# Expert tiles: gated rows turned one step later, second products two steps later, first products by half steps in three PSUM banks

## The reference

```python
x = x + 0.5 * ffn(layernorm(x))        # mixture of 8 experts, 2 chosen for each token
x = x + attention(layernorm(x))        # chunked delta-rule attention
x = x + 0.5 * ffn(layernorm(x))        # the same experts again

def ffn(xf):                           # for each expert e, w1 and w3: 256 x 128, w2: 128 x 256
    scores = softmax(xf @ gate_w); top_scores, top_idx = top_k(scores, 2)
    xs = scale[e] * xf                 # scale is the token's score for e, 0 if e was not chosen
    y += (silu(xs @ w1[e]) * (xs @ w3[e])) @ w2[e]
```

## Time and profile before

| | |
|---|---|
| median of three runs | 1602.56 us |
| profiled execution: span from first to last instruction | 1602.7 us |
| time around the span | none is given; the span is taken as the execution's time |
| TensorE busy (matrix multiplications) | 1349.0 us, 84% |
| VectorE / ScalarE / GpSimd busy | 1099.0 / 882.4 / 889.9 us |
| granted TensorE clock, mean | 0.929 of 2.4 GHz |
| gate function, 128x512, 72 times | 42.8 us busy, 154.3 us idle before it |

### The profile page before, as it was taken

How to read it: one execution, slowest core, us unless ns; L and a number is a source line. 1 busy time by engine, 2 the same in 40 slices (tenths; PEclk the granted TensorE clock), 3 DMA queues, 4 the chain that set the end, 5 groups by cost and what they waited for, 6 DMA issues and landing times. The chain is left out here.

```text
span 1602.7 us, 47314 instructions
## 1 busy us (share of the span) xinstructions
PE 1349.0 (84%) x17084; PEld 1208.4 (75%) x17084; DVE 1099.0 (69%) x2928; ACT 882.4 (55%) x1836; POOL 889.9 (56%) x1579
## 2 busy tenths in 40 slices
PE   7758888888557999999999999999997558878886
PEld 7757877877546888888888888878886457778775
DVE  7774454454376788989898998988984565543553
ACT  4424553455245777776676676676773335534552
POOL 3562455254536556657766676766757324562545
PEclk8978998998878999999999999999997779999998
DMA  8437663764101222222222222222223576537651
GB/s 249 161 115 228 215 202 122 266 212 159 57 22 25 42 51 47 52 60 71 74 63 68 67 70 64 75 70 65 71 56 81 169 222 221 192 152 246 207 179 60
DMA packets 218577, 193.42 MB, mean 121 GB/s; under 512 B 105188, under 2 KB 182250, under 8 KB 218352
## 3 DMA queue, kind: packets, MB, share of 16 engines
q1 hardware_dynamic: 184800, 114.06, 26.1%
q0 software_dynamic: 24576, 67.94, 11.5%
q10 hardware_dynamic: 8976, 8.40, 1.7%
HBM read 102.63 MB, written 94.01 MB: 123 GB/s over the span
## 5 line engine op out<-in xcount | busy, mean ns | idle before, releaser
L1734 DVE SCALAR_TENSOR_TENSOR raw_w<-attn_raw,taps,raw_w 128x256 f32<-128x256 f32 x576 | 240.9, 486 | 4.5 <-ACT raw_w L2143 4.5
L525 PE MATMUL ffn_both<-ws,ffn_xhi 128*128 x1152 | 211.7, 297 | 8.7 <-DVE ffn_xlo L743 3.8
L525 PEld LDWEIGHTS ffn_both<-ws,ffn_xhi 128*128 128x128 f32 x1152 | 170.9, 198 | 17.6 <-issue 17.2
L2421 POOL TENSOR_TENSOR attn_inv<-attn_inv,attn_term 64x14 f32<-64x14 f32 (+6 forms) x448 | 134.0, 299 | 35.1
L548 PE MATMUL ffn_yb<-ws,ffn_hhi 128*128 x576 | 132.0, 308 | 23.2 <-issue 14.7
L748 DVE TENSOR_TENSOR ffn_hid<-ffn_both,ffn_sil 128x512 f32<-128x512 f32 x72 | 49.6, 689 | 142.0 <-ACT ffn_sil L870 94.5
L2418 POOL TENSOR_TENSOR attn_term<-attn_small,attn_inv 64x14 f32<-64x14 f32 (+6 forms) x448 | 126.3, 282 | 32.6
L1334 PE MATMUL attn_fr<-attn_xhi,wqkv 128*128 128x256 f32 x768 | 139.3, 290 | 5.1 <-ACT attn_bth L2150 2.4
L870 ACT ACTIVATE ffn_sil<-ffn_both 128x512 f32<-128x512 f32 x72 | 42.8, 595 | 154.3 <-remote 108.0
L2460 POOL TENSOR_TENSOR attn_factors<-attn_squared,attn_powers 128x10 f32<-128x10 f32 x28 | 55.1, 1969 | 129.1 <-DVE attn_squared L1832 129.1
L548 PEld LDWEIGHTS ffn_yb<-ws,ffn_hhi 128*128 128x128 f32 x576 | 101.7, 204 | 32.8 <-issue 32.4
(11 more groups left out here) (342 smaller groups left out, 3904.0 us busy)
## 6 DMA issues: line engine op xcount, KB each, us to landing
ffn_xb<-second_rows SPq DMA_DIRECT2D x48, 259.0 KB
ffn_more_rows<-second_rows SPq DMA_DIRECT2D x48, 259.0 KB
raw_w<-second_rows SPq DMA_DIRECT2D x40, 259.0 KB
ffn_more_rows<-first_rows SPq DMA_DIRECT2D x64, 131.0 KB, 2.1
attn_xin<-x_after_first ACTq DMA_DIRECT2D x32, 256.0 KB, 2.7
attn_xres<-x_after_first SPq DMA_DIRECT2D x32, 256.0 KB
x_after_attention<-attn_xres SPq DMA_DIRECT2D x32, 256.0 KB
attn_xg<-x_after_attention SPq DMA_DIRECT2D x32, 256.0 KB, 3.1
```

The source lines that it names most:

```text
L525: last = pe.matmul(hp[:, j, :], (xhi, xlo)[b][:, k % 2, q, j * P:(j + 1) * P], ws[:, bass.ds(experts[j], 1), a, q].rearrange("p o d -> p ( ...
L1734: dve.scalar_tensor_tensor(acc[:, j, r], raw[:, j, r, :, tap:tap + P], taps[:, j, r, tap:tap + 1], acc[:, j, r], ALU.mult, ALU.add)\
L2421: pool.tensor_tensor(v[:, j + 1:, 0:j], v[:, j + 1:, 0:j], term[:, 0:k, 0:j], ALU.subtract)\
```

## The change

TensorE turns the gated rows of a step one step later and makes its second products two steps later. The first products are made in two half steps of two tiles each, each into one of three PSUM banks in turn (the third bank is `pos`, used only while tokens are being sent to experts). The gate function and the product with it are made by halves too, VectorE's and ScalarE's orders follow, and there are nine row buffers; the ninth takes the place of `xT`, which is used only while tokens are being sent to experts.

```diff
-        NW = 8
+        NW = 9
...
-        sil = sb("sil", [P, TPB, HF])
+        sil = sb("sil", [P, 2, TPB // 2, HF])
...
-        hp = both[:, 1].rearrange("p c t -> p (c t)").rearrange("p (j d) -> p j d", j=TPB)
+        hp = [t.rearrange("p (j d) -> p j d", j=TPB // 2) for t in (both[:, 1, 0], both[:, 1, 1], pos[:])]
...
             def up(k, experts, head):
-                wait(pe, sil_ready, k)
-                wait(pe, hid_ready, k)
+                wait(pe, hid_ready, 2 * k - 2)
...
                 for j in range(TPB):
-                    if head and j == TPB // 2:
-                        turn_rows(k + 1)
+                    n = 2 * k + j // 2
+                    if j == TPB // 2:
+                        if head:
+                            turn_rows(k + 1)
+                        wait(pe, hid_ready, n - 2)
...
-                last.then_inc(up_done, 1)
+                    if j % 2 == 1:
+                        last.then_inc(up_done, 1)
 
             def turn_hidden(k):
-                pe.wait_ge(hid_ready, k + 1)
+                pe.wait_ge(hid_ready, 2 * k + 2)
...
                     up(k, now, k == start)
+                    if k > start:
+                        turn_hidden(k - 1)
                     if k + 2 < end:
                         turn_rows(k + 2)
-                    if k > start:
-                        down(k - 1, of)
-                    turn_hidden(k)
-                    of = now
-                down(end - 1, of)
+                    if k > start + 1:
+                        down(k - 2, of[0])
+                    of = (of + [now])[-2:]
+                turn_hidden(end - 1)
+                down(end - 2, of[0])
+                down(end - 1, of[1])
...
                 for k in range(start, end):
-                    hidden(k)
+                    for h in range(2):
+                        hidden(k, h)
                     if k > start:
-                        results(k - 1)
+                        low_hidden(k - 1)
                     if k + 2 < end:
                         goals(k + 2)
                         low_part(k + 2)
-                    low_hidden(k)
+                    if k > start + 1:
+                        results(k - 2)
...
+                low_hidden(end - 1)
+                results(end - 2)
                 results(end - 1)
...
                 for k in range(start, end):
-                    silu(k)
+                    for h in range(2):
+                        silu(k, h)
+                    if k > start:
+                        high_hidden(k - 1)
                     if k + 2 < end:
                         high_part(k + 2)
                     if k + 3 < end:
                         scaled(k + 3)
-                    high_hidden(k)
...
+                high_hidden(end - 1)
```

More of the change, by code:

```diff
@@ L253, in ffn @@
         normed_lg = sb("normed_lg", [P, GB, E])
-        xT = sb("xT", [P, 2, KC, TB])
+        xT_room = sb("xT", [P, TPB * WIDE])
+        xT = xT_room[:, 0:2 * KC * TB].rearrange("p (h c t) -> p h c t", h=2, c=KC)
         lmax = sb("lmax", [P, GB])
@@ L276, in ffn @@
         slots = sb("slots", [P, 2, GB], I32)
-        past, skipped = (xT[:].rearrange("p h c t -> p (h c t)")[:, n * NTL * (E - 1):(n + 1) * NTL * (E - 1)]
+        past, skipped = (xT_room[:, n * NTL * (E - 1):(n + 1) * NTL * (E - 1)]
                          .rearrange("p (r t e) -> p r t e", r=2, e=E - 1) for n in range(2))
@@ L288, in ffn @@
             [raw_w[:, k * TPB * WIDE:(k + 1) * TPB * WIDE] for k in range(2)] +
-            [flat[:, 2 * TPB * DM + k * TPB * WIDE:2 * TPB * DM + (k + 1) * TPB * WIDE] for k in range(3)])]
+            [flat[:, 2 * TPB * DM + k * TPB * WIDE:2 * TPB * DM + (k + 1) * TPB * WIDE] for k in range(3)] +
+            [xT_room[:]])]
         xhi = sb("xhi", [P, 2, KC, TB], F32R)
@@ L510, in up @@
             def up(k, experts, head):
-                wait(pe, sil_ready, k)
-                wait(pe, hid_ready, k)
+                wait(pe, hid_ready, 2 * k - 2)
                 if head:
                     for _ in range(6):
-                        pe.matmul(hp[:, 0, 0:P], ident[:], ident[:], start=True, stop=True, skip_group_check=True)
+                        pe.matmul(hp[2 * k % 3][:, 0, 0:P], ident[:], ident[:], start=True, stop=True,
+                                  skip_group_check=True)
                 pe.wait_ge(xhi_ready, k + 1)
@@ L520, in up @@
                 for j in range(TPB):
-                    if head and j == TPB // 2:
-                        turn_rows(k + 1)
+                    n = 2 * k + j // 2
[3 more added lines that the diff above has]
+                        wait(pe, hid_ready, n - 2)
                     for t, (a, b) in enumerate(TERMS):
                         for q in range(KC):
-                            last = pe.matmul(hp[:, j, :], (xhi, xlo)[b][:, k % 2, q, j * P:(j + 1) * P],
+                            last = pe.matmul(hp[n % 3][:, j % 2, :], (xhi, xlo)[b][:, k % 2, q, j * P:(j + 1) * P],
                                              ws[:, bass.ds(experts[j], 1), a, q].rearrange("p o d -> p (o d)"),
@@ L577, in _ @@
                 turn_rows(start)
-                of = None
+                of = []
                 for k in range(start, end):
@@ L741, in low_part, with hidden @@
                 dve.wait_ge(xhi_ready, k + 1)
-                wait(dve, up_done, k - 1)
+                wait(dve, up_done, 2 * (k - 1))
                 dve.tensor_tensor(xlo[:, k % 2], tr, xhi[:, k % 2].bitcast(F32), ALU.subtract).then_inc(xlo_ready, 1)
-            def hidden(k):
-                dve.wait_ge(sil_ready, k + 1)
+            def hidden(k, h):
+                n = 2 * k + h
+                dve.wait_ge(sil_ready, n + 1)
                 wait(dve, hT_done, k - 1)
-                dve.tensor_tensor(hid[:, k % 2], hp[:, :, HF:], sil[:], ALU.mult).then_inc(hid_ready, 1)
+                dve.tensor_tensor(hid[:, k % 2, 2 * h:2 * h + 2], hp[n % 3][:, :, HF:], sil[:, h], ALU.mult)\
+                   .then_inc(hid_ready, 1)
             def low_hidden(k):
@@ L863, in high_part, with silu @@
                 act.wait_ge(tr_done, k + 1)
-                wait(act, up_done, k - 1)
+                wait(act, up_done, 2 * (k - 1))
                 act.activation(xhi[:, k % 2], tr, ACT.Copy).then_inc(xhi_ready, 1)
-            def silu(k):
-                act.wait_ge(up_done, k + 1)
-                wait(act, hid_ready, k)
-                act.activation(sil[:], hp[:, :, 0:HF], ACT.Silu).then_inc(sil_ready, 1)
+            def silu(k, h):
+                n = 2 * k + h
+                act.wait_ge(up_done, n + 1)
+                wait(act, hid_ready, n - 1)
+                act.activation(sil[:, h], hp[n % 3][:, :, 0:HF], ACT.Silu).then_inc(sil_ready, 1)
             def high_hidden(k):
```

## The result

The changed kernel takes 1636.68 us (median of four runs, 1618.24 to 1640.97), the kernel before 1602.26 beside it: 1.0183 times as long [1.0150, 1.0216], so slower by 1.8%, clear of the noise; 1586 had been forecast, in a range of 1532 to 1636. The profiled execution took 1640.97 us with a span of 1639.1, 36.4 over that of before.

The account below looks back on a forecast made before the run. The prediction took the loop of put, 5.83 us of held TensorE signals, and results to set 7.39 us a step, no engine being full. From 1602.7, 36.7 saved in steps less 20.5 for filling gave 1586 us, range 1532 to 1636.

Parts of the forecast that it names:

- Part 1, the gate signal off TensorE's path: TensorE, second products two steps later: it runs ahead until it needs the result buffer, free of the late gate signal (8.87 us interval).
- Part 2, VectorE's order: VectorE's order becomes hid, hlo, xlo, results, so a put depends on one more held signal, that of the row transposes.
- the hold: TensorE's signals during a put reach other engines late, until 5.8 us after a single put's start, 11.8 after a pair's.
- Part 3, half steps: Gate function and product by halves cost 0.17 us more on ScalarE, 0.16 on VectorE a step; taken as nothing in free time.
- Part 5, filling: Start of each half: first put comes after the third step's products, 5.1 us later, 20.5 in all (14 to 24).
- The drain: End of each half: the last two puts follow each other as before (5.16 us), so priced at nothing.
- The steady step: Puts come in back-to-back pairs of 13.4 to 13.9 us; 6.85 a step instead of 7.39 saves 36.7 us over 68.
- A: Rival: row transposes' signal waits for the pair's end; 15.6 us for two steps, 1651 us or 1619; chance 0.26.
- C: Rival: about even, pairs of both kinds, 7.02 to 7.16 us a step, 1598 to 1607 us; chance 0.10.
- D: Rival: GpSimd becomes the bound, puts in threes and more, 5.9 us a step, 1522 us; chance 0.10.
- E: Rival: no hold from GpSimd, by the state buffer page; TensorE's 5.98 us a step, 1527 us; chance 0.03.
- B: Rival: the put's loop stays at 7.39 us a step and only filling is added, 1623 us; chance 0.14.

## Why the prediction was wrong, point by point

- **What bounds the kernel.** For the chip of the main measurement the reading stood up: late starts beside scatters, and at the same distance, 5.75 us, on the chip with 1592 us. On four other chips there is no such lateness and TensorE sets 5.6 us. That the late starts go with scatters is shown (every "remote" wait in five traces ends beside one); that issuing the scatters causes them is not, since the same scatters do nothing on the other chips, and what they write to HBM runs at the same time.
- **Part 1, the gate signal off TensorE's path.** This fell first. TensorE no longer waits for that signal, but VectorE does: hid stands ahead of the results in its fixed order, and hid waits for the gate function. The signals were released 10.3 and 11.8 us after the pair's start, and the results stood behind them. "TensorE can run ahead" failed as well: its own instructions came piecemeal inside the second put (65.0 us of such waits before weight loads of second products, 36.7 before the change).
- **Part 2, VectorE's order.** Named as the risk, and rightly. Behind the late signal stand 4.5 us to the next put where the forecast had 0.05 + 1.55: 11.8 + 4.5 = 16.3, not 13.4. That putting the results first would save it is not shown: the only such run on a chip with the hold had pairs of 17.0 us, other signals being late.
- **Part 3, half steps.** Priced at nothing; 0.6% faster, together with part 4, where TensorE sets the step. Not tried with the hold. **Part 4, nine buffers:** priced at nothing, never tried by itself.
- **Part 5, filling.** 5.1 us a half forecast; 5.9, 5.1 and 5.1 measured, and 9.3 across the attention block, 25.4 in all for 20.5. It is the one cost that shows on both kinds of chip (3.3, 5.1, 2.6 and 3.5 on the faster). The drain, priced at nothing, was right in effect: three runs that reordered it gained nothing by it.
- **The steady step.** This is the step that failed: 6.7 to 7.0 us a step forecast, 7.55 measured. The pairs came as forecast, but the sum for a pair, 11.8 + 0.05 + 1.55 = 13.4, let the results follow the end of the hold at once. It left out that VectorE still waits for the gate function's held signal, with hid, hlo and xlo ahead of the results; measured are 11.8 + 4.5 = 16.3. The rows of before already had a pair with hid alone ahead of the results, 5.89 + 8.87 = 14.8 us, the same as two single puts of 7.4: even at that cost pairs gain nothing, and at 16.3 each loses 1.5. 11.1 us lost in place of 36.7 gained accounts for 47.8 of the 52.6 us between the forecast's span (1602.7 + 20.5 - 36.7 = 1586.5) and 1639.1; filling's 4.9 is the rest.
- **The rivals.** A came nearest, with 15.6 for a pair and its results behind a held signal, xlo's length and all; but the held one was the first products' and not the transposes', and hid and hlo stood in the row too. C was even, D and E don't occur on that chip; on the others E's statement (no hold) is what the traces show, and the change is slower there all the same (1.0084), because before has no hold to lose either. B's sum, the step as it was and filling on top, comes nearest to what happens there, though TensorE and not the put's loop sets that step.
- **The range.** It ended at 1636, with two pairs in three of kind A; 1636.68 lies just above. That it came so near is no merit of the sum: the pair had been mis-sized by 2.9 us.

What stays open: what makes the signals late and why only on some chips; whether it is the issuing of the scatters or their writes; whether fewer scatters would end it; how much of a pair's 16.3 us is TensorE's own second products being late; how much of the 11.1 us is the lower clock after a stall and how much VectorE's order.

## What to carry to other kernels

A stage made one step deeper costs one step wherever the loop starts anew behind a barrier, here 5.1 to 5.9 us where it could be read alone on the slower kind of chip and 3.3 to 5.1 on the faster, and pays only if the cycle that sets the step gets shorter; reordering the first or the last step alone didn't bring it back. Taking a consumer off one engine's path is not enough when another engine still serves it, in a fixed order, ahead of what the path needs: follow the moved instruction through every in-order queue. And before building on a wait that the profile can only call "remote", profile the same kernel once more on another chip: here the wait that the whole forecast rested on was absent on four of the five chips met afterwards.

## What the runs showed of the hardware

- The same kernel takes 1455 to 1457 us on four chips and 1592 and 1602 in two other measurements (9 to 10% more). In the slower trace of the changed kernel ScalarE's longest wait (9.3 us) ends 7.6 us after its products are recorded as over (1604.35 to 1611.90), with scatters running; on the faster ones it starts as they end (1394.70, transposes over at 1394.66), with the same scatters running.
- In the five traces of the slower kind every wait that no instruction's end explains ended while an indirect scatter ran or within 2.0 us after it; the fifteen traces of the faster kind have no such wait.
- On the slower kind TensorE's own instructions pause inside a put (0.34, 0.97 and 0.85 us in one step); on the faster one it is busy 75.00 of 75.00 us.
- A stretch with TensorE busy 2.64 of 4.90 us (granted clock 0.83) was followed by one at a granted clock of 0.51, the level of 1.2 GHz, in which first products took 5.2 us instead of 3.0.
- A put of four indirect scatters occupies GpSimd for 5.16 us, 1.29 from start to start, on both kinds of chip; one of two takes 2.58.
